# Expert feed-forward blocks around attention: dispatched rows carry residual and token weight, and expert outputs are scattered as finished rows

## The reference

```python
x = L0_attn_states
x = x + 0.5 * _L0_ffn_ref(_layernorm(x), gate_w, w1, b1, w2, b2)
x = x + _L0_attn_ref(_layernorm(x), Wq, bq, Wk, bk, Wv, bv, Wo, bo)
x = x + 0.5 * _L0_ffn_ref(_layernorm(x), gate_w, w1, b1, w2, b2)

# _L0_ffn_ref, E = 8, DFF = 512, T = 2048
probs = softmax(tokens @ gate_w.T)
expert_idx = argmax(probs)
capacity = ceil(1.25 * T / E)              # 320
keep = rank of the token within its expert < capacity
h = relu(dispatch @ w1[e] + b1[e])
expert_out = h @ w2[e] + b2[e]
ans = probs[expert] * expert_out           # 0 for tokens over capacity
```

## Time and profile before

| | us |
|---|---|
| median of the runs | 530.07 |
| lowest, highest of three | 529.17, 533.33 |
| the profiled execution: device time | 530.07 |
| the profiled execution: span, first to last instruction | 528.3 |
| TensorE busy (share of the span) | 416.6 (79%) |
| VectorE busy | 304.6 (58%) |
| ScalarE busy | 254.5 (48%) |
| POOL busy | 254.4 (48%) |
| mean granted TensorE clock | 0.925 |

### The profile page before, as it was taken

One profiled execution on the slowest core, in us unless ns is written; L12 is line 12 of the kernel. 1 busy time (PEld: TensorE's weight loads), 2 busy tenths in 40 slices (PEclk: granted clock), 3 DMA queues, 4 the chain that ended last, 5 costly groups with the idle time before them and its releaser, 6 DMA issues.

```text
span 528.3 us, 11673 instructions
## 1 busy us (share of the span) xinstructions
PE 416.6 (79%) x4337; PEld 287.9 (54%) x4337; DVE 304.6 (58%) x926; ACT 254.5 (48%) x441; POOL 254.4 (48%) x277
## 2 busy tenths in 40 slices
PE   1702999409799999999899999899999772299960
PEld 1601777305466766566575666665757442167850
DVE  5872345638967767378864598763888605012213
ACT  1100434007487888477865677684787310034310
POOL 6471245713665565266456565555565520205550
PEclk9999999858799999999999999999999886579995
DMA  7811343172000000000000000000000000125415
GB/s 271 281 54 53 114 134 117 37 257 84 1 2 1 1 4 1 1 2 2 1 2 6 17 2 2 2 1 21 3 2 2 1 20 0 57 59 158 128 53 166
DMA packets 31515, 28.06 MB, mean 53 GB/s; under 512 B 2732, under 2 KB 27365, under 8 KB 31208
## 3 DMA queue, kind: packets, MB, share of 16 engines
q1 hardware_dynamic: 27184, 19.97, 12.6%
q0 software_dynamic: 2560, 4.74, 2.7%
q10 hardware_dynamic: 1720, 2.66, 1.4%
HBM read 16.84 MB, written 10.52 MB: 52 GB/s over the span
## 4 chain that ended last, share of the span: by engine, by line
PE 58%; DVE 15%; POOL 11%; issue 7%; DMA 7%; ACT 1%; POOLq 1%; DVEq 0%; SPq 0%; ACTq 0%
PE sc L697 12%; PE sc L580 7%; PE pj L590 6%; PE pj L667 6%; PE tT L734 4%; POOL disp L330 4%; DVE Ph L1057 3%; PE cx L717 3%; PE cx L719 3%; PE sc L702 3%; PE cx L718 3%; PE pj L677 3%; PE tT L542 3%; DMA ytok<-empty 3%; POOL ytok L341 2%
## 5 line engine op out<-in xcount | busy, mean ns | idle before, releaser
L358 POOL TENSOR_TENSOR Pl<-Pf,Ph 128x512 f16<-128x512 f32 (+1 forms) x64 | 61.9, 980 | 75.4 <-DVE Ph L1057 75.4
L697 PE MATMUL sc<-Tq,Tk 64*128 64x128 f32 (+3 forms) x512 | 96.0, 473 | 0.0
L341 POOL DMA_INDIRECT ytok<-Y,who x48 | 48.6, 1012 | 71.5 <-DVE Y L925 59.2
L358 POOL TENSOR_TENSOR Pl<-Wf,Ph 128x512 f16<-128x512 f32 (+1 forms) x64 | 58.4, 928 | 48.7 <-DVE Ph L1057 48.7
L1057 DVE CAST Ph<-Pf 128x512 f16<-128x512 f32 (+1 forms) x96 | 55.2, 606 | 42.0 <-ACT Pf L491 41.2
L431 ACT ACTIVATE hT<-sc,RT 128x320 f32<-128x320 f32 x64 | 33.8, 528 | 93.2 <-PE sc L580 92.4
L717 PE MATMUL cx<-Vh,Ph 128*128 128x65 f16 x640 | 66.9, 197 | 14.5 <-POOL Vl L358 10.3
L717 PEld LDWEIGHTS cx<-Vh,Ph 128*128 128x128 f16 x640 | 59.9, 99 | 16.7 <-POOL Vl L358 11.5
L718 PE MATMUL cx<-Vl,Ph 128*128 128x64 f16 x640 | 67.0, 195 | 0.0
L719 PE MATMUL cx<-Vh,Pl 128*128 128x65 f16 x640 | 66.7, 195 | 0.0
L1057 DVE CAST Ph<-Wf 128x512 f16<-128x512 f32 (+1 forms) x96 | 53.7, 591 | 19.6 <-ACT Wf L491 19.1
(11 more groups left out here) (179 smaller groups left out, 842.6 us busy)
## 6 DMA issues: line engine op xcount, KB each, us to landing
W<-in_L_ffn_w SPq DMA_DIRECT2D x32, 256.0 KB
disp<-empty SPq DMA_DIRECT2D x2, 1290.0 KB, 7.7
XE<-disp SPq DMA_DIRECT2D x16, 129.0 KB
ytok<-empty SPq DMA_DIRECT2D x2, 1024.0 KB, 12.7
G<-ytok SPq DMA_DIRECT2D x8, 256.0 KB, 4.0
out<-X SPq DMA_DIRECT2D x4, 256.0 KB, 2.4
ytok<-Y,who POOLq DMA_INDIRECT x48
XE<-disp SPq DMA_DIRECT2D x16, 32.2 KB
```

The costliest lines, as they stand in the source:

```text
L341: pool.indirect_dma_start(ytok[phase], bass.IndirectOffsetOnAxis(ap=who[u][0:m, j:j + 1], axis=0), Y[u][0:m, j, :], None).then_inc(y_sc[u] ...
L358: pool.tensor_tensor(dst, src, hi, ALU.subtract).then_inc(done, 1)
L697: mm(score_bank(h, c)[:, o:o + w], Tk[u][half(h), P * kt:P * kt + P], Tq[u][half(h), P * kt:GN], start=kt == kts[0], stop=False)
```

## The change

Rows in `disp` and `XN` grow from 129 to 258 values: 128 normalised ones, the token's number, its weight (half the gate's probability, 0 over capacity) and the 128 values of the residual. `X` is now a view on the last 128 of `XN`, and `XN` keeps all 16 tiles in phase 1 too. `place` writes the weight into the row and only then lets POOL dispatch. An expert's output is finished in slot order: VectorE adds the bias as before, waits for its own result, and computes output x weight + residual with three more instructions, from `XE`. POOL scatters the finished rows: in phase 0 into `xmid`, which holds a copy of x beforehand (one DMA of 1 MB from `X`), and in phase 1 straight into the output, which got each group's `X` beforehand, so that tokens over capacity keep their residual; rows of empty slots fall out by the bound check there. The scatter takes its indices from `XE` itself. So `who`, `nxt`, `G`, `wts`, the combine, the gather and the output's write after phase 1 go; after phase 0 the gather remains and brings the new `X` from `xmid`.

`XE` has four buffers instead of two, and one is free only when its expert's scatter has landed: SP loads the first four experts' tokens at once, and those of e+2, for e = 2 to 5, after the scatter of e-2, behind the weight loads in its queue. The slots are filled by two DMAs now, a head of 130 values a row (520 bytes) and 128 zeros (512 bytes), with a pitch of 1,032 bytes; `ytok` and its fill go. The loops over experts are written out on all engines, and POOL's `passed` increment goes from its experts.

```diff
 NS = len(FIRST)
-ROW = P + 1
+NUM, WT, RES, ROW = P, P + 1, P + 2, 2 * P + 2
+HEAD = RES
...
-        ytok = [nc.dram_tensor(f"ytok{k}", [NTOK + SLOTS, P], F32, kind="Internal").ap() for k in range(2)]
+        xmid = nc.dram_tensor("xmid", [NTOK + SLOTS, P], F32, kind="Internal").ap()
...
         out_v = out.rearrange("b s d -> (b s) d").rearrange("(t p) d -> p t d", p=P)
...
-
-
-        X = sb("X", [P, NT, P], F32)
+        out_rows = out.rearrange("b s d -> (b s) d")
+        xmid_v = xmid[0:NTOK, :].rearrange("(t p) d -> p t d", p=P)
...
         XN = sb("XN", [P, NT, ROW], F32)
+        X = XN[:, :, RES:ROW]
         xa = sb("xa", [P, GT, P], F32)
-        G = sb("G", [P, NT, P], F32)
...
-        wts = sb("wts", [P, NT], F32)
...
-        XE = [sb(f"XE{u}", [P, 3, ROW], F32) for u in range(2)]
-        nxt = [sb(f"nxt{u}", [P, 3], U32) for u in range(2)]
-        who = [sb(f"who{u}", [P, 3], U32) for u in range(2)]
+        XE = [sb(f"XE{v}", [P, 3, ROW], F32) for v in range(NXE)]
...
+        def scattered_by(n):
+
+            return y_sc[n % 2], 48 * (n // 2 + 1)
...
+            def load_tokens(e, phase):
+                d, v = disp[phase], e % NXE
+                sp.dma_start(XE[v][:, 0:2, :], d[e * CAP:e * CAP + 2 * P, :].rearrange("(p j) d -> p j d", j=2)).then_inc(xe_in[v], 16)
+                sp.dma_start(XE[v][0:CAP - 2 * P, 2, :], d[e * CAP + 2 * P:(e + 1) * CAP, :]).then_inc(xe_in[v], 16)
 
             def fill(phase):
 
-                sp.dma_start(disp[phase][0:SLOTS, :].rearrange("(p j) d -> p j d", p=P), empty[:]).then_inc(S["slots_empty"], 16)
-                sp.dma_start(ytok[phase][0:NTOK, :].rearrange("(p j) d -> p j d", p=P), empty[:, 0:NT, 0:P]).then_inc(S["slots_empty"], 16)
+                sp.dma_start(disp[phase][0:SLOTS, 0:HEAD].rearrange("(p j) d -> p j d", p=P), empty[:]).then_inc(S["slots_empty"], 16)
+                sp.dma_start(disp[phase][0:SLOTS, RES:ROW].rearrange("(p j) d -> p j d", p=P), empty[:, :, 0:P]).then_inc(S["slots_empty"], 16)
 
             for k, (t0, tiles) in enumerate(FIRST):
                 sp.dma_start(X[:, t0:t0 + tiles, :], x_v[:, t0:t0 + tiles, :]).then_inc(x_in[k], 16)
+            sp.wait_ge(S["consts"], 2)
+            fill(0)
             for phase in range(2):
...
-                    sp.wait_ge(S["consts"], 2)
-                    fill(0)
-                for u in range(2):
...
                 if phase:
                     fill(1)
+                    for g in range(NG):
+                        sp.wait_ge(S["x_added"], g + 1)
+                        sp.dma_start(out_v[:, GT * g:GT * g + GT, :], X[:, GT * g:GT * g + GT, :]).then_inc(S["rows_kept"], 16)
+                else:
+                    for k in range(NS):
+                        sp.wait_ge(x_in[k], 16)
+                    sp.dma_start(xmid_v, X[:]).then_inc(S["rows_kept"], 16)
                 sp.wait_ge(S["scattered"], 16 * NT * (phase + 1))
-                load_tokens(0, 0, phase)
-                load_tokens(1, 1, phase)
-                n0 = E * phase
-
-                def first_layer(e, u):
-
-                    sp.wait_ge(S["xe_ready"], n0 + e + 1)
-                    load_tokens(e + 2, u, phase)
-                    sp.wait_ge(S["h_ps"], FT * (n0 + e + 1))
-                    load_w1(e + 2, u)
-
-                def second_layer(e, u):
-
-                    sp.wait_ge(S["y_ps"], n0 + e + 1)
-                    load_w2(e + 2, u)
-
-                first_layer(0, 0)
...
+                for e in range(E):
+                    if e + 2 < E:
+                        sp.wait_ge(S["h_ps"], FT * (n0 + e + 1))
+                        load_w1(e + 2)
+                    if 1 <= e < E - 1:
+                        sp.wait_ge(S["y_ps"], n0 + e)
+                        load_w2(e + 1)
+                    if e >= 2 and e + 2 < E:
+                        sp.wait_ge(*scattered_by(n0 + e - 2))
+                        load_tokens(e + 2, phase)
+                for e in range(E - 2, E):
+                    sp.wait_ge(*scattered_by(n0 + e))
+                if not phase:
+                    for g in range(NG):
+                        sp.dma_start(X[:, GT * g:GT * g + GT, :], xmid_v[:, GT * g:GT * g + GT, :]).then_inc(gsem[g], 16)
 
...
-                with pool.Fori(0, E // 2) as ee:
-                    for u in range(2):
-                        pool.wait_ge(S["y_ready"], E * phase + 2 * ee + u + 1)
-                        pool.sem_inc(S["passed"], 1)
-                        for j in range(3):
-                            m = min(P, CAP - P * j)
-                            pool.indirect_dma_start(ytok[phase], bass.IndirectOffsetOnAxis(ap=who[u][0:m, j:j + 1], axis=0),
-                                                    Y[u][0:m, j, :], None).then_inc(y_sc[u], 16)
+                rows, kept = ((xmid, 16), (out_rows, 16 * (NG + 1)))[phase]
+                pool.wait_ge(S["rows_kept"], kept)
+                for e in range(E):
+                    pool.wait_ge(S["y_ready"], E * phase + e + 1)
+                    for j in range(3):
+                        m = min(P, CAP - P * j)
+                        pool.indirect_dma_start(rows, bass.IndirectOffsetOnAxis(ap=XE[e % NXE][0:m, j, NUM:WT].bitcast(U32), axis=0),
+                                                Y[e % 2][0:m, j, :], None, bounds_check=(NTOK + SLOTS, NTOK)[phase] - 1,
+                                                oob_is_err=False).then_inc(y_sc[e % 2], 16)
...
+                def tokens(e):
+                    v = e % NXE
+                    pe.wait_ge(xe_in[v], 32 * (E // NXE * phase + e // NXE + 1))
...
+                def outputs(e):
+
+                    pe.wait_ge(w2_in[e % 2], 16 * (loads + e // 2 + 1))
+                    if e >= 2:
+                        pe.wait_ge(S["y_bias"], n0 + e - 1)
+                    ybank = (pj0, pj1)[e % 2]
...
+                tokens(0)
+                hidden(0)
+                tokens(1)
+                for e in range(E):
+                    if e + 1 < E:
+                        hidden(e + 1)
+                    if e + 2 < E:
+                        tokens(e + 2)
+                    outputs(e)
...
-                dve.tensor_tensor(idx[:, a], sk[:, a], tok[:, tiles_at], ALU.add).then_inc(S["idx_ready"], 1)
+                dve.tensor_tensor(idx[:, tiles_at], sk[:, a], tok[:, tiles_at], ALU.add)
...
                 dve.wait_ge(S["el_ready"], n + 1)
                 s.done(dve.tensor_reduce(se[:, a], el[:, a], X_AXIS, ALU.add))
                 s.done(dve.reciprocal(pr[:, a], se[:, a]))
-                s.done(dve.scalar_tensor_tensor(wts[:, tiles_at], pr[:, a], 0.5, keep[:, a], ALU.mult, ALU.mult))
+                dve.scalar_tensor_tensor(XN[:, tiles_at, WT], pr[:, a], 0.5, keep[:, a], ALU.mult, ALU.mult).then_inc(S["idx_ready"], 1)
...
+                def outputs(e):
+                    n, u, v = n0 + e, e % 2, e % NXE
                     yb = (pj0, pj1)[u]
+                    bias = b2bc[:, P * e:P * e + P]
                     dve.wait_ge(S["y_ps"], n + 1)
-                    bias = b2bc[:, bass.ds(P * e, P)]
+                    if n >= 2:
+                        dve.wait_ge(*scattered_by(n - 2))
                     dve.tensor_tensor(Y[u][:, 0:2, :], yb[:, 0:2 * P].rearrange("p (j d) -> p j d", j=2),
                                       bias.unsqueeze(1).broadcast_to([P, 2, P]), ALU.add)
-                    dve.tensor_tensor(Y[u][0:m, 2, :], yb[0:m, 2 * P:3 * P], b2bc[0:m, bass.ds(P * e, P)],
-                                      ALU.add).then_inc(S["y_ready"], 1)
+                    dve.tensor_tensor(Y[u][0:m, 2, :], yb[0:m, 2 * P:3 * P], b2bc[0:m, P * e:P * e + P],
+                                      ALU.add).then_inc(S["y_bias"], 1)
+                    dve.wait_ge(S["y_bias"], n + 1)
+                    for j, k in enumerate((P, P, m)):
+                        last = dve.scalar_tensor_tensor(Y[u][0:k, j, :], Y[u][0:k, j, :], XE[v][0:k, j, WT:RES],
+                                                        XE[v][0:k, j, RES:ROW], ALU.mult, ALU.add)
+                    last.then_inc(S["y_ready"], 1)
...
+                tokens(0)
+                tokens(1)
+                for e in range(E):
+                    if e + 2 < E:
+                        tokens(e + 2)
+                    if phase == 0:
+                        split_weights(e)
+                    outputs(e)
...
-            dve.tensor_copy(XN[:, :, P:ROW].rearrange("p t a -> p (t a)").bitcast(U32), number[:])
+            dve.tensor_copy(XN[:, :, NUM].bitcast(U32), number[:])
...
-                combine(0, g)
-                dve.wait_ge(S["combined"], g + 1)
+                dve.wait_ge(gsem[g], 16)
                 ln_stats(NS + g, GT * g, 0, GT)
...
             def norm_batch(n, g):
                 ln_scale(NS + NG - 1 + n, 0, GT)
-                dve.wait_ge(S["scattered"], 16 * (NT + GT * g))
```

(59 more changed lines are left out.)

118 lines of the change are left out of this document (37 added, 81 removed).

## The result

The kernel after takes 558.37 us (median of 4 runs, 556.35 to 560.04), the kernel before beside it 529.62 (4 runs, 526.89 to 533.33). The ratio is 1.055, 95% interval 1.051 to 1.060: slower by 5.5%. The profiled execution has a span of 556.9, 28.6 more than before's 528.3.

What follows compares the result with a forecast made beforehand. TensorE was taken as nearly full in attention and the expert stages, with serial work deciding at the start, hand-overs and end. From the 528.3 us span, seven terms gave 530.1, plus 1.77 made 531.9; range 522 to 539.

Steps and rivals of the forecast that it cites:

- step 6: Expert stages: buffers held until scatters land stall TensorE before tokens(4) and (6), not (5) and (7), each phase; +9.4 us.
- step 7: Expert stages: two of four stalls bring TensorE to half clock, each costing 1.5 us; +3.0 us.
- Step 4: Start: filling the slots in short pieces, costed by bytes at 278 GB/s, delays POOL's first dispatch; +2.6 us.
- Step 1: End of phase 1: gather, combine and output write go, multiply-adds and a short program end are added; -9.1 us.
- Step 2: Between phase 0 and attention: the first combine goes (-1.14), multiply-adds delay the scatters (+0.7); -0.4 us.
- Step 3: Attention's ramp: without three combines, TensorE's wait for Vl nearly vanishes and its half clock ends; -4.8 us.
- what is late next: Attention's ramp: once Vl is on time, the second normalise is late, by some 1.1 us.
- the fill goes by pieces: Rival at the start: fill time follows pieces, not bytes; +8 instead of +2.6 us, 537.3 in all; chance 0.13.
- Step 5: Into phase 1's experts: index waits for weight (+0.51), larger rows lengthen last dispatch and first token load (0.6); +1.1 us.

## Why the prediction was wrong

The mechanisms were nearly all named; 26.8 us lie between the sums. The step that failed by most is 6, the stalls for the token buffers, with step 7, the clock behind them: 12.4 us forecast, 26.4 measured. Step 4, the fill, comes next. By its steps:

- **Step 1 (-9.1; measured -3.8).** The term that failed is "some 0.35 remains for the program to end". The 0.88 of the multiply-adds (0.87) and the 0 for the bound check (0.98 against 0.96 a call) were right. POOL's drain, 6.6 us after its last indirect call, became the last thing. It ended at 523.29 in the trace before, under the combine and the output's write, where I did not look for it. With plain writes in place of the scatters the end is 4.63 instead of 13.47, and POOL's drain no longer closes it.
- **Step 2 (-0.4; measured -0.33).** The size was right by luck and the working wrong. The first combine's 1.14 was to arrive whole; it lay under POOL's 7 us after its last call, and without it alone nothing is gained. Nor did the multiply-adds delay the gather by 0.7: from phase 0's last product to the gather's issue it went from 9.44 to 9.54. The -0.33 is POOL's delay, 6.99 instead of 7.32, within its own 6.8 to 7.5.
- **Step 3 (-4.8; -2.62).** The term that failed is the wait, with "POOL's lows aren't stretched" as its reason: they hardly had been, for its four take 5.93 in the kernel without the three combines against 6.06 in the earlier trace rows's kernel. So Vl is not on time; TensorE waits 1.63 for it, not 0.2, and 1.3 are gained there instead of 2.7. The clock holds after a wait of that length, as forecast; it and what is late next give 1.4 where 3.2 - 1.1 was set down.
- **Step 4 (+2.6; +8.75).** The term that failed is the rate of the new fill, 278 GB/s at a share of 1.0, taken from short pieces of another kind (the output's write). The fill of the kernel after moves 176 at a share of 1.22, which is 144 at 1.0 (an estimate by the prediction's own scaling); the kernel before's short pieces move 312 at 1.03. So the new pieces cost about twice what the old ones did, and neither bytes nor their number alone gives that. The size is that of the rival "the fill goes by pieces", at +8; its reason is only part of it. Its "against", that a share of 1.0 means that bytes count, was the wrong reading: the engines are as full at 176 as at 416.
- **Step 5 (+0.5 for the weight, +0.6 for the larger rows).** `idx` to weight is 0.5 as forecast. In the stretch's sum (-0.82) it can't be seen; a part of that stretch differs by up to 2.7 between traces with no edit there. The larger rows gave +1.07 here, but +0.2 to +0.3 in the five other traces with the same loads, so about half of the estimate and within what one execution differs from another.
- **Step 6 (+9.4; 16.1).** The step that failed is "tokens(5) is on time, since the stall moved it too", and what it left out: it asked what is queued behind the tokens' load, and not what that load is queued behind. The stall moved outputs(2) as well, and SP loads tokens(5) behind W2(4), which waits for the end of outputs(2); tokens(6) and (7) come behind W2(5) and W2(6) in the same way. With the two exchanged the trace shows the forecast pattern, 1.9 to 2.6 where 2.1 to 2.5 was forecast.
- **Step 7 (+3.0; 7.3 in the outputs).** Half of the stalls brought half clock, as assumed, but there were eight and not four. The shortest after which it came was 1.50 (tokens(5), phase 1), which the earlier trace rows's 1.8 without a fall had seemed to exclude; 2.06, 1.77, 2.39 and 2.10 were not followed by it. So length alone does not tell. Each cost 1.5 to 2.6.
- The two stages grew by 26.4; 16.1 of stalls and 7.3 in the outputs make 23.4. Some 0.8 of the other 3.0 lies at the start of phase 0's stage and is there with eight buffers too (58.3 against 57.4). The remaining 2.1 lie at the eight stalls, 0.6 at the first and 0.2 at each of the others: without a wait the transposes start some 0.16 us before the recorded end of the hidden products (82.78 against 80.53 + 2.42 with eight buffers), and the times in brackets don't count that.

Steps 6 and 7 together were forecast at 12.4 and the stages gave 26.4, 14 more; step 4 gave 6.2 more, step 1 5.3, step 3 2.2. Each of the errors is on the same side: where something was hidden (the drain, POOL's turn to another kind of work, SP's order) I had taken it as absent.

## What to carry to other kernels

When a buffer is to be held longer, follow its reload through the whole in-order queue that issues it, once with the stalls it makes put in; if there is memory, the extra buffers (12 KB a partition here) are worth more than the order. Before a tail is costed at its removal, look for what already ends under it: an engine's drain or a turn of POOL is seen only in the sequencer's rows. A fill or a copy is costed by a row whose pieces have the same length, distance and start, and a full DMA share says nothing about bytes.

## What the runs showed of the hardware

- POOL after indirect DMAs: the next pow starts 6.8 to 7.5 us after the last call's end, even where its input is there over a microsecond before (seven traces), and the program's drain ends 6.6 us after it (in all eight traces in which scatters are its last calls; 4.6 where the last calls were dispatches, some 60 us before the end).
- Fills of HBM: 2.65 MB in 5,120 runs of 512 and 520 bytes, 1,032 bytes apart, run at 176 GB/s with the engines' share at 1.22, in 256 runs of 10 KB at 416 with a share of 0.99; runs of 512 bytes without a gap at 312 with 1.03. The Trainium skill (DMA: Bandwidth & Descriptors, Specifications) puts the bound for line rate at 512 B. The 176 GB/s disagree with it, since no run there is shorter; what beside the length sets the rate is not shown.
- TensorE's clock comes back at different points in traces where the code of the stretch is the same. At phase 1's first experts the first 16 hidden products took 4.61 and 4.05 us in before's profile, and 3.81 and 2.42 in that of the kernel without the first combine. The stretch from the first query product of attention's last step to the last batch's first dispatch took 48.3 to 48.6 in four traces and 45.6 in four others, the kernel after 47.9; the granted clock in it was 0.82 in the kernel before and 0.85 with eight buffers. The four at 45.6 are the four runs on one chip, so this may be the chip's and not the execution's. That is up to 2.7 us twice, or 1% of the time, with no edit in either place.
